# Paged attention in a four-layer decoder: four page buffers in place of three, and less of Wo kept early

## The reference, cut to what matters

```python
q = rope(rmsnorm(x @ Wq.T))            # 32 heads of 128
k = rope(rmsnorm(x @ Wk.T))            # 8 heads of 128
v = x @ Wv.T
kc = k_cache[block_table]              # 16 pages of 32 keys for each of 64 sequences
vc = v_cache[block_table]
k_all, v_all = concat([kc, k]), concat([vc, v])        # 544 keys
probs = softmax(where(valid, q @ k_all.T / sqrt(128), -1e30))
x = x + (probs @ v_all) @ Wo.T         # Wo is 512 x 4096
x = x + ...                            # three more layers
```

## Time and profile before

| what | us |
|---|---|
| median of three runs (lowest to highest) | 2230.19 (2223.37 to 2231.25) |
| the profiled execution, its own time | 2221.79 |
| its span, first to last instruction | 2220.0 |
| TensorE busy in the span | 2152.6 |
| VectorE busy | 1462.8 |
| ScalarE busy | 1392.3 |
| GpSimd busy | 220.3 |
| granted clock of TensorE, mean | 0.997 of full |

### The profile page before, as it was taken

The page is one execution under the profiler, slowest core; times in us unless marked ns, Lnnn a source line. Parts: engine busy times, 40 slices in busy tenths (PEclk is TensorE's granted clock), DMA queues, the critical chain, the costliest instruction groups (busy, mean ns, idle before and its releaser), DMA issues.

```text
span 2220.0 us, 77529 instructions
## 1 busy us (share of the span) xinstructions
PE 2152.6 (97%) x30576; PEld 1647.3 (74%) x30576; DVE 1462.8 (66%) x3642; ACT 1392.3 (63%) x4174; POOL 220.3 (10%) x208
## 2 busy tenths in 40 slices
PE   8999999999999999999999999999999999999998
PEld 6888888887666766667676676676777888888886
DVE  5799999994566766667676666666764433433433
ACT  4888888884677777777777777777773222222221
POOL 5211111110000111100000000000003101101101
PEclk9999999999999999999999999999999999999999
DMA  5455545548999999999999999999984333333331
GB/s 193 104 131 113 115 110 117 132 97 272 359 338 319 324 330 317 312 321 329 334 323 319 323 309 328 314 316 308 335 295 145 107 90 101 107 95 101 98 101 50
DMA packets 355010, 490.22 MB, mean 221 GB/s; under 512 B 58994, under 2 KB 191346, under 8 KB 351987
## 3 DMA queue, kind: packets, MB, share of 16 engines
q1 hardware_dynamic: 354674, 485.62, 68.3%
HBM read 397.37 MB, written 88.08 MB: 219 GB/s over the span
## 4 chain that ended last, share of the span: by engine, by line
PE 94%; issue 2%; SPq 2%; DMA 1%; DVE 1%; ACT 1%; ACTq 0%; DVEq 0%
PE o_bank L971 25%; PE s_bank L951 23%; PE acc L730 8%; PE acc L731 8%; PE acc L732 8%; PE proj L1408 5%; PE proj L1410 5%; PE proj L1409 5%; PE wide L1455 1%; PE wide L1450 1%; PE slim L1439 1%; PE wide L1451 1%; PE turn L1429 1%; PE slim L1437 1%; DMA kv<-k_spill 0%
## 5 line engine op out<-in xcount | busy, mean ns | idle before, releaser
L971 PEld LDWEIGHTS o_bank<-p_t,kv 32*128 32x128 f32 x17408 | 519.5, 187 | 134.0 <-issue 132.8
L898 DVE CUSTOM_DVE_ANT_0 probs<-s_bank,mask 128x544 f32<-128x544 f32 x512 | 370.7, 725 | 356.3 <-PE s_bank L951 356.3
L971 PE MATMUL o_bank<-p_t,kv 32*128 32x128 f32 x17408 | 574.8, 277 | 23.5 <-issue 22.7
L951 PE MATMUL s_bank<-kv,q_t 128*32 128x288 f32 (+1 forms) x8192 | 531.3, 397 | 22.7 <-issue 20.6
L856 ACT ACTIVATE probs<-probs,neg_max 128x544 f32<-128x544 f32 x512 | 383.4, 752 | 258.5 <-DVE neg_max L898 246.7
L951 PEld LDWEIGHTS s_bank<-kv,q_t 128*32 128x32 f32 x8192 | 247.7, 110 | 217.1 <-issue 32.4
L912 DVE STREAM_TRANSPOSE p_t<-probs 128x544 f32<-128x544 f32 x512 | 365.3, 731 | 0.4 <-ACT probs L862 0.4
L862 ACT ACTIVATE probs<-probs,inv_sum 128x544 f32<-128x544 f32 x512 | 356.8, 751 | 0.0
L730 PE MATMUL acc<-w_hi,x_hi 128*128 128x512 f32 x764 | 300.5, 393 | 0.0
L731 PE MATMUL acc<-w_lo,x_hi 128*128 128x512 f32 x764 | 300.1, 393 | 0.0
L732 PE MATMUL acc<-w_hi,x_lo 128*128 128x512 f32 x764 | 298.1, 390 | 0.0
(11 more groups left out here) (137 smaller groups left out, 2466.7 us busy)
## 6 DMA issues: line engine op xcount, KB each, us to landing
kv<-in_kv_pages SPq DMA_DIRECT2D x1024, 256.0 KB, 4.6
q_spill<-stage SPq DMA_DIRECT2D x512, 64.0 KB, 1.8
q_t<-q_spill SPq DMA_DIRECT2D x64, 512.0 KB, 5.8
o_spill<-o_t SPq DMA_DIRECT2D x64, 512.0 KB, 6.6
raw<-o_spill SPq DMA_DIRECT2D x64, 512.0 KB, 3.5
kv<-in_w_qkv SPq DMA_DIRECT2D x11, 1024.0 KB, 5.8
v_spill<-stage SPq DMA_DIRECT2D x8, 1024.0 KB, 7.1
k_spill<-stage SPq DMA_DIRECT2D x128, 64.0 KB, 1.8
```

The lines of the kernel that those rows point to most:

```text
L898: nc.vector.tensor_tensor_reduce(out=probs[:, i], in0=s_run(n), in1=mask[:, b % 2], scale=-SCALE, scalar=3.0e38, op0=ALU.add, op1=ALU.min, ...
L951: last = pe.matmul(s_banks[n % 2][rows, columns].rearrange("p (s t) -> p s t", t=PSIZE), q_t[:, b % 2, g, r * S:(r + 1) * S], kv[:, buf, s ...
L971: last = pe.matmul(o_banks[a][:, hh * ROWS:(hh + 1) * ROWS], kv[rows, buf, c, VALUES + hh * HD:VALUES + (hh + 1) * HD], p_t[rows, m % 2, c ...
```

## The change: the diff

BUFS becomes 4 and `buf_of(b)` is b modulo 4. `x_lo` of project moves into the fourth page buffer, and the stage buffer into `wo_early`. SP's loop asks in iteration b for pages and own keys and values of batch b, as before, but for the queries of batch b - 1; the queries of the last batch and one more store follow after the loop. WO_EARLY goes from 16 to 8 (two loads, in iterations 4 and 5) and HI_EARLY from 16 to 6. `wo_late` then has 24 heads and spans two page buffers; `o_hi` and `o_lo` stand in the third.

```diff
-BUFS = 3
+BUFS = 4
-WO_EARLY = 16
-HI_EARLY = 16
+WO_EARLY = 8
+HI_EARLY = 6
 def buf_of(b):
-    return (b + BUFS - 1) % BUFS
+    return b % BUFS
             x1 = after("x1", [P, D])
-            assert place[0] <= kv_start + BUF_BYTES
             o_hi_done, o_split = sem("o_hi_done"), sem("o_split")
-            place = [kv_start + BUF_BYTES]
-            o_hi = nc.alloc_sbuf_tensor_at("o_hi", [P, 2, CH, P], F32R, offset=place[0])
-            place[0] += 2 * CH * P * 4
...
+            up2, up2_lo = after("up2", [2 * LOWS, D], "up2_lo")
+            assert place[0] <= kv_start + 2 * BUF_BYTES
+            place = [kv_start + 2 * BUF_BYTES]
+            o_hi = nc.alloc_sbuf_tensor_at("o_hi", [P, 2, CH, P], F32R, offset=place[0])
+            place[0] += 2 * CH * P * 4
             o_lo = nc.alloc_sbuf_tensor_at("o_lo", [P, 2, CH, P], F32R, offset=place[0])
             place[0] += 2 * CH * P * 4
-            up2, up2_lo = after("up2", [2 * LOWS, D], "up2_lo")
-            assert place[0] <= kv_start + 2 * BUF_BYTES
...
-        x_lo = nc.alloc_sbuf_tensor_at("x_lo", [P, DC, TOK], F32R, offset=wo_start)
+        x_lo = nc.alloc_sbuf_tensor_at("x_lo", [P, DC, TOK], F32R, offset=kv_start + buf_of(3) * SLOTS * PAGE * 4)
+        stage = wo_early[:, :, :].rearrange("p h n -> p (h n)").rearrange("p (i n) -> p i n", i=2)
...
-        stage = sb("stage", [P, 2, QUARTER * SLICE])
...
-        WO_WITH = {b: HS * (b - 2) for b in range(2, 2 + WO_EARLY // HS)}
+        WO_WITH = {b: HS * (b - BUFS) for b in range(BUFS, BUFS + WO_EARLY // HS)}
...
             sp.wait_ge(projected, NSL * NT)
-            load_pages(sp, 2)
             for b in range(2, B):
                 if b == BUFS:
                     for i in range(2):
                         sp.wait_ge(stored[i], 16 * (NV + (NQ + NK) * NT) * (NT // QUARTER) // 2)
                 if b >= BUFS:
                     sp.wait_ge(summed, 4 * (b - BUFS + 1))
-                if b > 2:
-                    load_pages(sp, b)
+                load_pages(sp, b)
                 load_own_keys(sp, b)
                 load_own_values(sp, b)
-                sp.wait_ge(scored, (b - 1) * HK)
-                load_queries(sp, b)
+                if b > 2:
+                    sp.wait_ge(scored, (b - 2) * HK)
+                    load_queries(sp, b - 1)
                 if b in WO_WITH:
                     h = WO_WITH[b]
                     sp.dma_start(wo_early[:, h:h + HS], wo_t[:, h:h + HS, :]).then_inc(wo_in, 16)
                 if b >= BUFS:
                     store(b - BUFS)
+            sp.wait_ge(scored, (B - 2) * HK)
+            load_queries(sp, B - 1)
+            store(B - 4)
             sp.wait_ge(summed, 4 * (B - 2))
             load_late(sp)
             store(B - 3)
...
-        CHUNK_AFTER = {FIRST_PIECE + 3: 2, FIRST_PIECE + 5: 3}
+        CHUNK_AFTER = {FIRST_PIECE + 4: 2, FIRST_PIECE + 8: 3}
```

## The result

The changed kernel took 2238.99 us (median of 7 runs, 2225.85 to 2246.1) against 2223.62 us of the kernel before on the same chip (7 runs, 2217.33 to 2231.25). The ratio is 1.0058, 95% interval [1.0034, 1.0082]: slower, by some 13 us by the ratio and by 15.4 us between the medians. Run again later it gave 2233.59 against 2224.8 us, 1.0042 [1.0018, 1.0065], some 9 us. The profiled execution of after took 2226.0 us, at the low end of its runs, so this trace shows the places of the loss better than its full size.

The account below looks back on a forecast made before the run. TensorE, busy in 97% of the span, was taken as the bound, with transfers close to it in attend. Terms +6.4 - 1.0 + 0 = +5.4 us took 2230.2 to 2235.6, predicted as 2236 us, 80% range 2220 to 2247.

Parts of the forecast that it names:

- The place and the size of the hole: Start of attend: queries 2 land behind pages 3, so TensorE idles +9.0 us ahead of batch 2, bounds +7.8 and +12.
- The steady state: Later batches of attend: same cycle of waits, batches wait for queries and not pages, 17.3 us a batch, gain 0.
- The rival of deeper pages: Attend: pages land last at most starts, so more lead removes 16.8 us, 2218.8 us or down to 2180; chance 0.12.
- What comes back of the hole: Batches 2 to 6: some 2.6 of the 9.0 us come back, leaving +6.4 us at batch 6.
- two limits: Start of batch 6: queue lands queries 6 at 653.2 us, TensorE arrives at 654.5; the later one counts.
- The end of attend: Last two batches: no further pages asked for and queries 63 go out earlier, -1.0 us, bounds 0 and 1.7.
- the cover: The late Wo load, 18.1 us long, ends at 1648.5 and is wanted only after 1660: 12 us to spare.
- The split in finish: Finish: five more pieces for ScalarE and VectorE, which stays just ahead of TensorE: 0, bounds 0 and +2 us.
- The sum: Whole kernel: +6.4 - 1.0 + 0 = +5.4 us, from 2230.2 to 2235.6 us.
- the likeliest case: The forecast itself for the whole kernel: +5.4 us, 2236 us, own range 2232 to 2241; chance 0.47.
- The second rival: Batches 2 to 6: the hole stays and widens, queries 5 and 6 late behind Wo loads, +15 us, 2245; chance 0.23.

Follow-up runs that it names:

- q_mid4: The changed kernel with the queries of batch b - 1 asked for in the middle of the pages of batch b: 2219.5 us, ratio 0.9979.
- q_mid3: The kernel before, three buffers, with the queries of batch b asked for in the middle of its own pages: 2214.3 us, ratio 0.9955.
- mid3_in4: loop3_in4 with the queries asked for in the middle of the pages of their own batch: 2208.8 us, ratio 0.9942.
- q2_first: The changed kernel with only queries 2 asked for ahead of pages 3: 2232.7 us, ratio 1.0032.
- wo_at_8: The changed kernel with its two loads of Wo in iterations 8 and 9 in place of 4 and 5: 2231.7 us, ratio 1.0046.
- q2_first_wo8: The changed kernel with queries 2 ahead of pages 3 and the loads of Wo in iterations 8 and 9: 2225.9 us, ratio 1.0024.
- before_again: The kernel before, unaltered, run again for a second trace: 2217.5 us, ratio 0.9973.
- loop3_in4: The changed kernel's memory layout and Wo part with SP's loop of the kernel before, so without the lead: 2221.2 us, ratio 1.0010.
- lead_at_32: loop3_in4 up to iteration 31, then the changed kernel's loop, a batch ahead, from iteration 32 on: 2232.6 us, ratio 1.0055.

## Why the prediction was right, and where it was off

**The place and the size of the hole: right.** I had +9.0 us of idle time ahead of batch 2 at 585.2; it was 9.14 us, batch 2 at 586.35 (585.1 in the second trace), with queries 2 issued at 579.23 where I had about 580. In the second trace it was 7.95 us, near the lower bound of 7.8.

**The steady state: right.** The cycle of waits is the same with the names shifted by one. Score waits less the hole are 12.8 and 14.4 us, against 16.8 and 13.7; batches 6 to 61 take 963.7 and 964.8 us against 969.8 and 955.5. The rival of deeper pages is out. That queries and not pages are last is shown by q_mid4, q_mid3 and mid3_in4, where moving the queries alone leaves 0 to 1.7 us of idle time at batch starts, and by the landings in the traces. One reading was too generous: I took all 16 stretches of the earlier trace rows as batch starts that wait for data, and 5 of them, with 3.9 us, are inside batches and of the kind of the holes inside groups.

**What comes back of the hole: right in size, with a thinner reason.** I had +6.4 us at batch 6. Measured: 655.8 - 648.3 = 7.5 in the first traces, 654.4 - 649.0 = 5.4 in the second. I had named two limits there, 653.2 for the queue and 654.5 for TensorE. In the two traces of after queries 6 land at 655.2 and 654.2 us, and TensorE doesn't idle at all from 586.4 to 655.8 us in the first; in before it idled 4.5 us in the same batches. That idle time, less 1.8 us by which TensorE was busy for longer, is the 2.7 us that came back. (The 347 GB/s that I gave to batches 2 to 5 are of a row that begins with batch 3.) q2_first, wo_at_8 and q2_first_wo8 bear out that both are real: it takes both moves to bring batch 6 to 650.0. The step had an omission, 2.5 us of low clock behind the hole, and an error against it (last section).

**The end of attend: wrong in sign.** I took back 1.0 us. From the start of batch 62 to the first matmul of the Wo product were 41.2 and 42.0 us in the two traces of before and 42.5 and 42.8 in those of after: +1.0. I had counted the pages that are no longer asked for, and not that a load of 6 MB in place of 4 MB now runs just there (the DMA share from 1631 to 1652 us is 0.83, where it was 0.78). TensorE of after at the end of attend has holes inside groups, here while that load runs (1631.7 to 1651.8 us):

```profile
1641.47 1.29 PE L952 MATMUL s_bank<-kv,q_t 128*32 128x256 f32 x17 [0.59 <-issue]
...
1648.79 1.85 PE L972 MATMUL o_bank<-p_t,kv 32*128 32x128 f32 x57 [1.41 <-issue]
```

Before has them at the same places of the stream, and shorter:

```profile
1639.89 1.29 PE L951 MATMUL s_bank<-kv,q_t 128*32 128x256 f32 x17 [0.18 <-issue]
...
1646.11 1.85 PE L971 MATMUL o_bank<-p_t,kv 32*128 32x128 f32 x57 [0.31 <-issue]
```

These are instruction packets again. That the larger load makes them later is likely but not shown: before_again has 0.78 and 0.31 us there, and no run has the change with a smaller load. It isn't the lead that does it: loop3_in4, with the same load and no lead, takes 43.1 us here.

The load itself took 20.1 us from issue to landing by the profile's list of transfers, where I had 18.1; it was wanted 10 us later, so the cover held. The split in finish cost 0 as forecast, within 0.5 us: after its start, finish took 562.2 and 560.6 us against 560.7 and 561.3.

**The sum.** The mean spans of the two traces of each kernel are 2223.4 and 2213.9 us, +9.5, made of about 6.5 by batch 6, 1.6 in the steady state (inside its spread), 1.0 at the end and 0.4 in finish. I had +5.4. The runs say 9 and 13 us. So the direction and the mechanism of the hole were right, and the likeliest case was too small: of the missing 4 us the traces give 2.0 to the end of attend, and the rest is in the steady state's scatter, which I can't assign. That 2236 lies within 3 us of the measured 2239.0 is in part luck: I had counted from 2230.2 us, the median of three runs, and seven runs of the kernel before gave 2223.6; from there +5.4 us makes 2229.0, ten under the measurement. By chances I gave 0.64 to no measurable difference and 0.24 to slower; the two ratios, 1.0058 and 1.0042, stand on either side of the bound. The second rival had the hole stay whole with +15 us; its size is near the first ratio, but its mechanism, queries held up by the loads of Wo, is not what the trace of after shows: there the batches after the second run at 16.3 to 19.2 us and the start of batch 6 is only 5 to 8 us late.

## What to carry to other kernels

A deeper buffer pays only for what is late. Before adding one, find what the consumer's start waits for last in the queue; here it was 512 KB of queries behind 4.46 MB of pages and own rows, and moving them into the middle of the pages took 0.4 to 0.8% off, with three buffers and with four, while the fourth buffer's lead cost 0.4 to 0.6%. And a lead must be filled once. On a queue that is full at that place (a share of 1.0 and more) the fill was paid by TensorE each time: as one hole of 8 to 11 us at batch 2 or batch 32, or, with the queries moved ahead, spread over the next batches, so that batch 6 began 7 to 9 us later than in loop3_in4 or mid3_in4 either way.

## What the runs showed of the hardware that was not expected

A hole of 8 to 11 us costs more than its length, because TensorE's granted clock falls inside it. In the first score group behind the hole of after the 32 matmuls take 3.85 us, in lead_at_32 behind 10.91 us 3.73 us; behind the 2.44 us of idle time of the earlier trace rows they take 2.04. The kernel before pays it too, at batch 1, where the clock stands at 0.55 from 557 to 560 us:

```profile
557.01 3.34 PE L951 MATMUL s_bank<-kv,q_t 128*32 128x288 f32 x32 [3.53 <-issue]
```

Windows of after across the hole, columns as in the earlier trace rows:

```profile
577.00:581.00 4.00, 0.21 (x3) 0.01 (x1) 0.00 (x0) 0.24 (x1) 0.00 (x0) 1.00 1.05 386
581.00:586.00 5.00, 0.00 (x0) 0.00 (x0) 0.00 (x0) 0.00 (x0) 0.00 (x0) 0.53 1.06 343
586.00:591.00 5.00, 4.65 (x48) 2.44 (x52) 1.37 (x3) 0.84 (x2) 0.00 (x0) 0.50 1.06 388
591.00:596.00 5.00, 5.00 (x132) 3.85 (x132) 3.60 (x12) 3.21 (x7) 0.00 (x0) 0.94 1.06 368
```

The granted clock is still full up to 581 us, while TensorE idles, 0.53 from there to 586, 0.50 (the 1.2 GHz level) in the first 5 us of work, then nearly full again (0.94). Two groups are slow for it, by 3.85 - 2.04 = 1.8 and 2.73 - 2.07 = 0.7 us: 2.5 us that my working did not have. They didn't show in batch 6's start because the batches behind them ran faster than the steady 17.32 us that I had used: from 605.55 to 655.81 are 16.75 us a batch. Two errors cancelled there.

The instructions of an unrolled loop come by the same 16 transfer engines as the data. With the engines at 0.95 busy, 28 packets of them came late from batch 6 to 61, for 21.3 of TensorE's 34.3 us of idle time; at 0.66 it was 9 packets and 4.5 us. No semaphore names such a wait.

The transfers ran at 374 GB/s over the 28 us ahead of batch 2. The Trainium skill, "DMA: Bandwidth & Descriptors", Specifications, gives about 358 GB/s as the HBM side's limit for one core; this stretch stands above it, so for one core that runs alone the measured rate decides.
